# A mixture-of-experts tail in a language-model tower: coefficients applied in the expert blocks, block table computed one stage earlier

## The chip, the cores and the metric

The kernel runs on one core of a Trainium2 chip. The metric is the device time of one execution in microseconds (us). The engines are TensorE (PE in the profile, PEld its weight loads), VectorE (DVE), ScalarE (ACT), GpSimd (POOL) and SyncE (SP), which here only issues DMAs. On-chip memory is SBUF (128 partitions), matrix products land in the banks of PSUM, and everything that is passed between stages through memory outside the core goes through scratch tensors (`scratch_...`).

## The reference

Eight sequences of 512 tokens are embedded, run through a two-layer tower with banded attention, then through an induced-set attention block, and last through a two-level mixture of experts, which is the part that matters here:

```python
x = inp.reshape(-1, d)                     # 4096 tokens, d = 128
gw = _topk_gate(x @ wg_group, GK, G)       # 2 of 4 groups
z = _layernorm(x, ln_g, ln_b)
for g in range(G):
    iw = _topk_gate(z @ wg_inner[g], EK, E)    # 2 of 8 experts
    moe = jnp.zeros_like(z)
    for e in range(E):
        h = jax.nn.relu(z @ W1[g, e] + b1[g, e])
        moe = moe + iw[:, e:e + 1] * (h @ W2[g, e] + b2[g, e])
    y = _layernorm(z + moe, gln_g[g], gln_b[g])
    out = out + gw[:, g:g + 1] * y
return out + inp
```

Each token thus needs four expert rows, two for each of its two groups. The two of a group, weighted, and z are summed before a layernorm.

## The kernel before, in words

Four stages follow one another, each with its own program on every engine and a barrier between them: `embed`, `tower`, `induce`, `experts`. The change touches the last two.

**`induce`** works on eight items (sequences) in a software pipeline: a list of steps (`STEPS`), with 16 steps between items, and each engine runs for every step the pieces that are due in it. For an item m the gate is computed in the steps GATE to SLOT: VectorE's `coefficients` writes for each token its four expert coefficients and the 2 x 4 mixing weights of its groups into one tile `coef`, and `slots` the row of the scratch tensor `zs` for each of its four copies. GpSimd writes z and the token's number (column E) into the tile `z` with four copies of each token, and scatters them, 16 indirect DMAs for each item (L1440), so that the rows of one expert lie together in `zs`, in a region of its own. SyncE stores base, z and coef of each item to scratch tensors (L1375 to L1379). After the last item VectorE casts the counts of rows per expert (L1925), and SyncE and ScalarE write padding rows behind each region; GpSimd waits at the end for all scatters.

**`experts`** first loads constants (L1984), the coefficients (L1985), and on VectorE turns the counts into a table `tab` by a chain of 20 small operations (L2143 to L2164): for each of 95 blocks of 256 rows its expert and its first row in `zs`. Meanwhile TensorE transposes the mixing weights of all tokens (L2058), and ScalarE copies them to `mixed` (L2104). SyncE then goes through the blocks: two register loads from the table, a load of the expert's weights `w` (578 KB, six buffers) and one of the 256 rows (`rows`, 132 KB, six buffers, each reused when the scatter of six blocks before has landed). After block 4 (`if q == 4`) it also loads z and base of all tokens, 2 MB each.

For a block, TensorE transposes the rows (L2065), multiplies by W1 (L2077) and by W2 (L2089, one block behind). ScalarE copies the transposed rows (L2109) and applies bias and relu to one half of the hidden features (L2118), VectorE to the other (L2173). VectorE adds b2 (L2181) and GpSimd scatters the 256 results, two indirect DMAs (L2030), to `yt`, four rows for each token. The rows are not yet weighted.

When all scatters have landed, the **end** goes over the eight sequences, with two buffers `res` and two tiles `m`. SyncE loads the four result rows of each token (1 MB a sequence). VectorE multiplies rows 0 and 1 by their coefficients (L2190), GpSimd rows 2 and 3 (L2040). VectorE adds the two rows of each group (L2194) and z (L2195) and takes the statistics (L2201, L2204). GpSimd forms scale and shift in four small operations (L2043 to L2049), ScalarE normalises (L2129). TensorE multiplies the mixing weights with the group norms' gains and offsets (L2097); VectorE multiplies and adds (L2212, L2213, L2218, L2219), in the function `mixed_in`, which runs one sequence behind `gathered`.

Engines wait for each other by semaphores that count; `step` on VectorE waits for the operation just issued. PSUM banks go round in rings (`Tiles`) in an order that is a list of keys: in `up` the mixing keys stood first.

## Time and profile before

| | us |
|---|---|
| median of 3 runs | 2460.18 (2458.41 to 2463.89) |
| the profiled execution, its own time | 2446.1 |
| its span, first to last instruction | 2444.3 |
| TensorE busy in the span | 2019.2 (83%) |
| VectorE busy | 1323.6 (54%) |
| ScalarE busy | 1130.3 (46%) |
| GpSimd busy | 779.1 (32%) |

The profile is of one execution; its times are us from its first instruction. Busy time says how much an engine does, not whether anybody waits for it; that is read stage by stage, from windows of the span, and from a timeline: a list of instructions in order of time, merged where alike, with the idle time before each in brackets and what ended it. In a timeline `SPq` is the issue of a DMA by SyncE. The granted clock of TensorE is given as a share of 2.4 GHz: 0.50 is 1.2 GHz. The mean over the span is 0.88.

### The profile page before, as it was taken

The page shows a single profiled execution, that of the slowest core. Times are in us where ns is not written, and L with a number is a line of the kernel's source. Part 1 is how long each engine was busy: PE and PEld are TensorE (multiplying, and loading weights), DVE is VectorE, ACT ScalarE, POOL GpSimd, SP SyncE. Part 2 cuts the span into 40 slices and gives each one's busy share as a digit, 9 for nine tenths or more (in the row PEclk, how much of TensorE's full clock was granted, in tenths as well). Part 3 has the DMA queues.
Part 4 walks back from the last instruction along what each step waited for, and adds up shares of the span by engine and source line. Part 5 has one row for each costly group of instructions (what it writes and reads, how often), then busy time and mean ns, then how long its engine had stood idle before and what let it go on. Part 6 is the DMA issues. An engine that isn't in the chain of part 4 may idle for free. (4 is left out here: it accounts for less than half of the span.)

```text
span 2444.3 us, 43805 instructions
## 1 busy us (share of the span) xinstructions
PE 2019.2 (83%) x14601; PEld 1450.0 (59%) x14601; DVE 1323.6 (54%) x4329; ACT 1130.3 (46%) x2400; POOL 779.1 (32%) x975
## 2 busy tenths in 40 slices
PE   5799999999999999999995478867665179999944
PEld 4466666666666666666664356645443069999922
DVE  2365556656566555665562455776755223333358
ACT  2476656666666666665661134544432023333322
POOL 0012222222221222212222111235667625555543
PEclk7699999999999999999997566987776589999965
DMA  3641344213442144412400334522311477777622
GB/s 99 121 75 34 40 66 66 54 30 51 66 66 69 22 65 66 66 40 28 66 2 0 84 75 81 100 60 58 77 32 50 134 244 229 232 230 215 194 93 79
DMA packets 119393, 211.47 MB, mean 87 GB/s; under 512 B 23236, under 2 KB 52038, under 8 KB 118520
## 3 DMA queue, kind: packets, MB, share of 16 engines
q1 hardware_dynamic: 108024, 189.29, 34.9%
q0 software_dynamic: 10176, 17.09, 2.1%
q8 instruction: 124, 2.03, 0.4%
q10 hardware_dynamic: 976, 2.30, 0.3%
q14 instruction: 93, 0.76, 0.1%
HBM read 149.82 MB, written 66.82 MB: 89 GB/s over the span
## 5 line engine op out<-in xcount | busy, mean ns | idle before, releaser
L675 ACT ACTIVATE tower_prob<-tower_prob,tower_negmax 128x386 f32<-128x386 f32 (+1 forms) x768 | 390.5, 556 | 303.1 <-DVE tower_negmax L882 302.5
L882 DVE CUSTOM_DVE_ANT_0 tower_prob<-tower_sbank,tower_band 128x386 f32<-128x386 f32 (+1 forms) x768 | 346.4, 489 | 138.1 <-PE tower_sbank L449 132.9
L487 PEld LDWEIGHTS tower_tbank<-tower_ident,tower_prob 128*128 128x128 f32 x1920 | 227.6, 143 | 131.1 <-issue 81.0
L487 PE MATMUL tower_tbank<-tower_ident,tower_prob 128*128 128x128 f32 x1920 | 283.9, 278 | 23.2 <-DVE tower_probT L907 21.2
L731 ACT ACTIVATE tower_probT<-tower_tbank 128x384 f32<-128x384 f32 (+1 forms) x576 | 228.0, 431 | 126.3 <-PE tower_tbank L487 124.0
L2030 POOL DMA_INDIRECT scratch_yt<-experts_y,experts_rows x190 | 186.7, 983 | 202.4 <-DVE experts_y L2181 171.7
L426 PE MATMUL tower_dbank<-tower_oxT,tower_w 96*128 96x512 f32 x384 | 192.0, 625 | 12.1 <-ACT tower_oxT L720 12.0
L2089 PE MATMUL experts_ybank<-experts_w,experts_hid 128*128 128x128 f32 x1520 | 186.8, 277 | 0.0
L2118 ACT ACTIVATE experts_hid<-experts_hbank,experts_w 128x256 f32<-128x256 f32 x190 | 79.8, 471 | 224.4 <-PE experts_hbank L2077 224.4
L2077 PE MATMUL experts_hbank<-experts_zT,experts_w 128*128 128x256 f32 x760 | 182.1, 383 | 1.0 <-issue 1.0
L449 PE MATMUL tower_sbank<-tower_k_st,tower_q_st 49*128 49x386 f32 (+1 forms) x768 | 160.5, 412 | 26.3 <-POOL tower_k_st L631 13.6
L2089 PEld LDWEIGHTS experts_ybank<-experts_w,experts_hid 128*128 128x128 f32 x1520 | 178.9, 193 | 0.1
L2173 DVE TENSOR_SCALAR experts_hid<-experts_hbank,experts_w 128x256 f32<-128x256 f32 x190 | 83.2, 480 | 144.1 <-PE experts_hbank L2077 144.1
L647 POOL TENSOR_TENSOR tower_glob<-tower_vglob,tower_prob 128x102 f32<-128x102 f32 x128 | 46.5, 364 | 351.3 <-ACT tower_prob L675 227.5
L2077 PEld LDWEIGHTS experts_hbank<-experts_zT,experts_w 128*128 128x128 f32 x760 | 138.6, 193 | 16.9 <-issue 1.7
L346 PE MATMUL tower_dbank<-tower_w,tower_hid 128*128 128x192 f32 x768 | 140.7, 334 | 4.5 <-DVE tower_hid L857 4.5
L466 PE MATMUL tower_obank<-tower_probT,tower_v 128*17 128x128 f32 x3840 | 142.6, 275 | 0.7 <-ACT tower_probT L731 0.7
L1440 POOL DMA_INDIRECT scratch_zs<-induce_z,induce_slot x128 | 127.2, 994 | 38.4 <-issue 38.1
L365 PE MATMUL tower_dbank<-tower_xT,tower_wqk 96*96 96x512 f32 x256 | 131.9, 642 | 5.5 <-ACT tower_xT L690 5.5
L346 PEld LDWEIGHTS tower_dbank<-tower_w,tower_hid 128*128 128x128 f32 x768 | 123.1, 190 | 17.8 <-issue 10.9
L449 PEld LDWEIGHTS tower_sbank<-tower_k_st,tower_q_st 49*128 49x128 f32 x768 | 74.1, 185 | 94.4 <-issue 83.4
L1506 ACT ACTIVATE induce_probT<-induce_tbank 128x512 f32<-128x512 f32 x128 | 69.6, 597 | 96.8 <-PE induce_tbank L1145 56.3
(315 smaller groups left out, 3397.2 us busy)
## 6 DMA issues: line engine op xcount, KB each, us to landing
experts_w<-ew SPq DMA_DIRECT2D x95, 578.0 KB, 4.0
scratch_qk<-tower_qk SPq DMA_DIRECT2D x64, 384.0 KB, 4.7
tower_q_st<-scratch_qk SPq DMA_DIRECT2D x96, 192.0 KB, 8.2
tower_k_st<-scratch_qk SPq DMA_DIRECT2D x96, 192.0 KB, 11.2
experts_rows<-scratch_zs SPq DMA_DIRECT2D x95, 132.0 KB, 3.1
scratch_kq<-induce_kq SPq DMA_DIRECT2D x8, 1024.0 KB, 4.3
experts_res<-scratch_yt SPq DMA_DIRECT2D x8, 1024.0 KB, 5.6
induce_k_st<-scratch_kq SPq DMA_DIRECT2D x48, 128.0 KB, 4.3
```

The source lines that it names most:

```text
L346: mm = pe.matmul(bank[:, j * D:(j + 1) * D], lhs[:, k, t * P:t * P + P], rhs[:, k, :], start=(k == 0), stop=(k == kts - 1))
L365: mm = pe.matmul(bank[0:DP, :], wqk[layer][:, w, k, c * DP:c * DP + DP], xT[:, k, :], start=(k == 0), stop=(k == KT - 1))
L426: mm = pe.matmul(bank[:, :], w1[:, k, c * P:c * P + P], oxT[:, k, :], start=(k == 0), stop=(k == KT - 1))
L449: mm = pe.matmul(bank[:, 0:width(i)], stack(q_st[j], h0 + e)[:, i * P:i * P + P], stack(k_st[j], h0 + e)[:, first_key(i):first_key(i) + wi ...
L466: mm = pe.matmul(obank[32 * e:32 * e + W17, c:c + P], v[nq % 2][:, t, h0 + e, :], probT[(2 * gq + e) % PT][:, jb * P:jb * P + P], start=(j ...
L487: mm = pe.transpose(bank[:, jb * P:jb * P + P], prob[:, hg % PR, at + jb * P:at + jb * P + P], ident[:, :])
L675: act.activation(prob[:, hg % PR, 0:width(i)], prob[:, hg % PR, 0:width(i)], ACT.Exp, bias=negmax[:, hg % PR:hg % PR + 1], scale=-1.0).the ...
L731: turned.copied(act.activation(probT[(2 * (g - 1) + e) % PT][:, 0:at], bank[:, 0:at], ACT.Copy), ("t", g - 1, e))
L882: scores.copied(dve.tensor_tensor_reduce(prob[:, hg % PR, 0:width(i)], bank[:, 0:width(i)], band[:, BAND_AT[i]:BAND_AT[i] + width(i)], sca ...
L2030: pool.indirect_dma_start(out=a["yt"], out_offset=bass.IndirectOffsetOnAxis(ap=rows[q % ZB][:, h, E:E + 1].bitcast(U32), axis=0), in_=y[q ...
L2077: mm = pe.matmul(bank[:, j * TB:j * TB + TB], w[q % WW][:, W1 + c * P:W1 + c * P + P], zT[q % 2][:, :], start=True, stop=True)
L2089: mm = pe.matmul(bank[:, h * E:h * E + E], hid[q1 % 2][:, c, h * P:h * P + P], w[q1 % WW][:, W2 + c * E:W2 + c * E + E], start=(c == 0), s ...
```

## The change

Three things are done.

1. The four coefficients of a token travel with its rows: `coefficients` writes them to column E + 1 of the tile `z`, before the scatter. In a block, ScalarE forms half of the row's z (`zhalf`), and VectorE, after adding b2, forms y * coefficient + zhalf with two scalar_tensor_tensor, one for each 128 rows. A new semaphore `y_set` says that this is done; the scatter waits for it. The sum of a group's two rows then contains weights and z. z is no longer stored and loaded.
2. The block table is computed at the end of `induce`, behind the cast of the counts (L1925), with its constants loaded among that stage's late loads; table, counts and identity lie in tiles that outlive the stages. The mixing weights are loaded after block 4 and transposed after the last block.
3. At the end GpSimd alone adds the two rows of each group (`pair_sums`), one sequence ahead; there are four `res` buffers and three `m` tiles. VectorE keeps the statistics and the mixing.

The core of the diff (the 20 operations of the table are moved as they are):

```diff
@@ induce: coefficients on VectorE @@
-                    ins = dve.tensor_tensor(coef[:, :, SLOTS + j * G:SLOTS + j * G + G], outer_(hot),
+                    ins = dve.tensor_tensor(coef[:, :, j * G:j * G + G], outer_(hot),
                                             weights(4 - j)[:, :, G:G + 1].broadcast_to([P, NT, G]), ALU.mult)
-                step(ins)
-                dve.tensor_reduce(coef[:, :, 0:SLOTS], parts[:, :, :, :], AX.X, ALU.add).then_inc(coef_set, 1)
+                ins.then_inc(gates_set, 1)
+                dve.wait_ge(gates_set, m + 1)
+                dve.wait_ge(z_named, m + 1)
+                dve.tensor_reduce(z[m % 2][:, :, :, E + 1], parts[:, :, :, :], AX.X, ALU.add).then_inc(coef_set, 1)
@@ induce: stores on SyncE @@
-                        sp.wait_ge(z_ready, m + 1)
-                        sp.dma_start(a["z"][m], z[j][:, :, 0, 0:E]).then_inc(z_out, 16)
-                        sp.wait_ge(coef_set, m + 1)
+                        sp.wait_ge(gates_set, m + 1)
                         sp.dma_start(a["coef"][m], coef[:, :, :]).then_inc(coef_out, 16)
@@ induce: scatter on GpSimd @@
                             pool.wait_ge(z_copied, m + 1)
+                            pool.wait_ge(coef_set, m + 1)
...
-                            pool.wait_ge(z_out, 16 * (m - 1))
@@ induce: late loads @@
-                (grows, "grows"), (wgate, "wgate"), (rank, "rank"), (upper, "upper"), (ids, "ids0"))
+                (grows, "grows"), (wgate, "wgate"), (rank, "rank"), (upper, "upper"), (ids, "ids0"),
+                (steps, "steps"), (tri, "tri"), (origin, "count0"), (bidx, "iota"))
@@ induce: end of VectorE @@
             dve.tensor_copy(tail[:, :], count[0:1, :]).then_inc(tail_set, 1)
+            step(dve.tensor_tensor(blocks[:, :], count[:, :], origin[:, :], ALU.subtract))
...
+            dve.tensor_copy(tab[:, :], tabf[:, :]).then_inc(tab_set, 1)
+            dve.wait_ge(tab_set, 1)
@@ experts @@
-        WW, ZB, YB = 6, 6, 4
+        WW, ZB, YB, RB, MB = 6, 6, 4, 4, 3
...
-        res = [ph.sb(f"res{j}", [P, TC, SLOTS, E]) for j in range(2)]
-        m = [ph.sb(f"m{j}", [P, TC, 2, E]) for j in range(2)]
+        res = [ph.sb(f"res{j}", [P, TC, SLOTS, E]) for j in range(RB)]
+        m = [ph.sb(f"m{j}", [P, TC, 2, E]) for j in range(MB)]
...
-            for dst, src in consts:
-                sp.dma_start(dst[:], a[src]).then_inc(consts_in, 16)
-            sp.dma_start(coef[:, :, :].rearrange("p (r t) c -> p r (t c)", r=B),
-                         a["coef"].rearrange("r p t c -> p r (t c)")).then_inc(coef_in, 16)
-            sp.wait_ge(tab_set, 1)
             for q in range(NBLK):
...
                 if q == 4:
-                    sp.dma_start(z[:, :, :].rearrange("p (b t) d -> p b (t d)", b=B),
-                                 a["z"].rearrange("b p t d -> p b (t d)")).then_inc(base_in, 16)
+                    sp.dma_start(glmix[:, :], a["glmix"]).then_inc(consts_in, 16)
+                    sp.dma_start(coef[:, :, :].rearrange("p (r t) c -> p r (t c)", r=B),
+                                 a["coef"].rearrange("r p t c -> p r (t c)")).then_inc(coef_in, 16)
@@ experts: ScalarE, in each block @@
+                act.wait_ge(rows_in[q % ZB], 16 * (q // ZB + 1))
+                if q >= 2:
+                    act.wait_ge(y_set, q - 1)
+                act.activation(zhalf[q % 2][:, :, :], rows[q % ZB][:, :, 0:E], ACT.Copy, scale=0.5)\
+                    .then_inc(zhalf_set, 1)
@@ experts: VectorE, in each block @@
+                    down.wait_copied(dve, ("y", q1))
+                    dve.wait_ge(zhalf_set, q1 + 1)
+                    for h in range(HB):
+                        yh = y[q1 % YB][:, h, :]
+                        ins = dve.scalar_tensor_tensor(yh, yh, rows[q1 % ZB][:, h, E + 1:E + 2],
+                                                       zhalf[q1 % 2][:, h, :], ALU.mult, ALU.add)
+                    ins.then_inc(y_set, 1)
@@ experts: GpSimd, in each block @@
-                down.wait_copied(pool, ("y", q))
+                pool.wait_ge(y_set, q + 1)
@@ experts: GpSimd, the end @@
-            pool.wait_ge(coef_in, 16)
+            def pair_sums(b):
+                pool.wait_ge(res_in[b % RB], 16 * (b // RB + 1))
+                if b >= MB:
+                    pool.wait_ge(added, b - MB + 1)
+                pairs = res[b % RB][:, :, :, :].rearrange("p t (j k) d -> p t j k d", k=2)
+                pool.tensor_tensor(m[b % MB][:, :, :, :], pairs[:, :, :, 0, :], pairs[:, :, :, 1, :], ALU.add)\
+                    .then_inc(summed, 1)
+            pair_sums(0)
             for b in range(B):
-                pool.wait_ge(res_in[b % 2], 16 * (b // 2 + 1))
-                part = res[b % 2][:, :, 2:SLOTS, :]
-                pool.tensor_tensor(part, part, coef[:, TC * b:TC * b + TC, 2:SLOTS, None]
-                                   .broadcast_to([P, TC, 2, E]), ALU.mult).then_inc(scaled, 1)
+                if b + 1 < B:
+                    pair_sums(b + 1)
                 pool.wait_ge(moments, b + 1)
@@ experts: VectorE, the end (gathered) @@
-                dve.wait_ge(res_in[b % 2], 16 * (b // 2 + 1))
-                part = rb[:, :, 0:2, :]
-                step(dve.tensor_tensor(part, part, coef[:, TC * b:TC * b + TC, 0:2, None].broadcast_to([P, TC, 2, E]),
-                                       ALU.mult))
-                dve.wait_ge(scaled, b + 1)
-                pairs = rb[:, :, :, :].rearrange("p t (j k) d -> p t j k d", k=2)
-                step(dve.tensor_tensor(mb[:, :, :, :], pairs[:, :, :, 0, :], pairs[:, :, :, 1, :], ALU.add))
-                dve.tensor_tensor(mb[:, :, :, :], mb[:, :, :, :],
-                                  z[:, TC * b:TC * b + TC, None, :].broadcast_to([P, TC, 2, E]), ALU.add)\
-                    .then_inc(summed, 1)
                 dve.wait_ge(summed, b + 1)
```

Two places show how instructions move. The first is SyncE's program at the start of `experts`, before (constants, then `experts_tab` is read into registers):

```order
L1984 DMA experts_ident<-ident 128x128
L1984 DMA experts_glmix<-glmix 8x384
L1984 DMA experts_steps<-steps 128x16
L1984 DMA experts_tri<-tri 128x1024
L1984 DMA experts_origin<-count 128x32
L1984 DMA experts_bidx<-iota 128x1
L1985 DMA experts_coef<-scratch_coef 128x8x48
L1989 TENSOR_LOAD experts_tab
...
L1990 TENSOR_LOAD experts_tab
...
L1993 DMA experts_w<-ew 128x1156
```

and the same place with the change, where the table is called `sh_tab` (the last row of `induce` stands first):

```order
L1058 DMA scratch_zs<-padrows 16x2112
L924 UNCONDITIONAL_BRANCH
L2007 UNCONDITIONAL_BRANCH
L2010 TENSOR_LOAD sh_tab
...
L2011 TENSOR_LOAD sh_tab
...
L2014 DMA experts_w<-ew 128x1156
...
L2018 DMA experts_rows<-scratch_zs 128x264
```

Seven loads have gone from in front of the first weights. The second place is VectorE's program for one round of the end, before:

```order
L2190 TENSOR_TENSOR experts_res<-experts_res,experts_coef 128x4x256
L2194 TENSOR_TENSOR experts_m<-experts_res 128x1024
L2195 TENSOR_TENSOR experts_m<-experts_m,experts_z 128x1024
L2201 BN_STATS experts_st<-experts_m 128x6 x8
L2204 BN_AGGR experts_mv<-experts_st 128x2 x8
L2212 TENSOR_TENSOR experts_out<-experts_out,experts_hbank 128x128
```

and with the change, on VectorE and then, for one round, on GpSimd:

```order
L2222 TENSOR_TENSOR experts_out<-experts_out,experts_m 128x512
L2204 BN_STATS experts_st<-experts_m 128x6 x8
L2207 BN_AGGR experts_mv<-experts_st 128x2 x8
L2215 TENSOR_TENSOR experts_out<-experts_out,experts_hbank 128x128
L2216 TENSOR_TENSOR experts_m<-experts_m,experts_hbank 128x256
```

```order
L2064 TENSOR_TENSOR experts_m<-experts_res 128x1024
L2072 TENSOR_SCALAR experts_rstd<-experts_mv 128x8
L2074 TENSOR_TENSOR experts_rstd<-experts_rstd,experts_half 128x8
L2076 TENSOR_TENSOR experts_shift<-experts_rstd,experts_mv 128x8
L2078 TENSOR_SCALAR experts_shift<-experts_shift 128x8
```

Three operations of 1024 elements have left VectorE's round, and GpSimd's multiplication of that size has become the pair sum, which stands before the four small operations of the sequence one back.

## Rows read from the trace of the kernel before

**Rows 1.** Windows of blocks and of the end; first line names the columns
```profile
core 0: us, PE busy (x) PEld busy (x) DVE busy (x) ACT busy (x) POOL busy (x), PEclk, DMA share, GB/s
...
2000.00:2100.00 100.00, 100.00 (x699) 93.17 (x698) 34.70 (x80) 33.07 (x81) 52.90 (x54) 1.00 0.70 220
...
2345.00:2445.00 100.00, 38.38 (x56) 17.41 (x56) 84.61 (x232) 25.48 (x64) 40.38 (x40) 0.50 0.29 90
```
**Rows 2.** Timeline at the boundary: start us, duration us, engine, line, [idle before]
```profile
1913.45 0.16 DVE L1925 CAST induce_tail<-count 1x32 int32<-1x32 f32 x1
...
1944.39 0.96 POOL L1440 DMA_INDIRECT scratch_zs<-induce_z,induce_slot  x1 [0.30 <-issue]
...
1948.54 0.35 SPq L1984 DMA_DIRECT2D experts_ident<-ident  x1
...
1961.10 0.17 DVE L2164 CAST experts_tab<-experts_tabf 128x2 int32<-128x2 f32 x1
...
1962.77 0.38 SPq L1993 DMA_DIRECT2D experts_w<-ew  x1
...
1966.91 0.69 PE L2065 MATMUL experts_zbank<-experts_ident,experts_rows 128*128 128x128 f32 x2 [6.85 <-DMA experts_rows<-scratch_zs]
```
**Rows 3.** Timeline around the two large loads issued after block 4
```profile
1972.84 0.43 SPq L2000 DMA_DIRECT2D experts_z<-scratch_z  x1
...
1991.34 0.69 PE L2065 MATMUL experts_zbank<-experts_ident,experts_rows 128*128 128x128 f32 x2 [5.41 <-DMA experts_rows<-scratch_zs]
...
1997.32 0.38 PE L2065 MATMUL experts_zbank<-experts_ident,experts_rows 128*128 128x128 f32 x2
```
**Rows 4.** Windows of two stretches, columns as in rows 1
```profile
1952.00:1954.00 2.00, 0.00 (x0) 0.00 (x0) 0.20 (x2) 0.00 (x0) 0.00 (x0) 0.50 0.87 219
...
1986.00:1988.00 2.00, 0.00 (x0) 0.00 (x0) 0.88 (x2) 0.03 (x1) 1.46 (x2) 1.00 1.05 412
```
**Rows 5.** DMA issues in 1970 to 1995: count, KB each, us to landing
```profile
experts_z<-scratch_z SPq DMA_DIRECT2D x1, 2048.0 KB, 10.8
```
**Rows 6.** Timeline of one steady expert block
```profile
2326.23 0.88 DVE L2173 TENSOR_SCALAR experts_hid<-experts_hbank,experts_w 128x256 f32<-128x256 f32 x2 [1.41 <-PE experts_hbank L2077]
...
2326.35 0.38 ACT L2109 ACTIVATE experts_zT<-experts_zbank 128x256 f32<-128x256 f32 x1 [0.16 <-PE experts_zbank L2065]
...
2328.13 0.43 DVE L2181 TENSOR_TENSOR experts_y<-experts_ybank,experts_w 128x256 f32<-128x256 f32 x1 [1.03 <-PE experts_ybank L2089]
```
**Rows 7.** Timeline: VectorE's L1892 beside GpSimd, twice
```profile
1755.66 2.05 DVE L1892 SCALAR_TENSOR_TENSOR induce_gc<-induce_ga,induce_gates 128x160 f32<-128x160 f32 x1
...
1756.25 1.27 POOL L1483 TENSOR_TENSOR induce_base<-induce_h,induce_x 128x512 f32<-128x512 f32 x1
...
1903.47 1.03 POOL L1440 DMA_INDIRECT scratch_zs<-induce_z,induce_slot  x1 [0.30 <-issue]
...
1903.70 0.33 DVE L1892 SCALAR_TENSOR_TENSOR induce_gc<-induce_ga,induce_gates 128x160 f32<-128x160 f32 x1
```
**Rows 8.** Timeline of the end: first item, one round, last item
```profile
2344.57 1.23 DVE L2190 TENSOR_TENSOR experts_res<-experts_res,experts_coef 128x1024 f32<-128x1024 f32 x1 [10.71 <-DMA experts_res<-scratch_yt]
...
2377.59 2.41 POOL L2040 TENSOR_TENSOR experts_res<-experts_res,experts_coef 128x1024 f32<-128x1024 f32 x1
...
2378.17 2.92 DVE L2190 TENSOR_TENSOR experts_res<-experts_res,experts_coef 128x1024 f32<-128x1024 f32 x1
...
2383.64 1.64 DVE L2201 BATCH_NORM_STATS2 experts_st<-experts_m 128x6 f32<-128x128 f32 x8
...
2385.88 0.25 DVE L2212 TENSOR_TENSOR experts_out<-experts_out,experts_hbank 128x128 f32<-128x128 f32 x1
...
2389.01 3.18 ACT L2129 ACTIVATE experts_m<-experts_m,experts_shift,experts_rstd 128x128 f32<-128x128 f32 x8 [8.17 <-POOL experts_shift L2049]
...
2389.52 2.92 DVE L2190 TENSOR_TENSOR experts_res<-experts_res,experts_coef 128x1024 f32<-128x1024 f32 x1
...
2437.89 0.29 DVE L2212 TENSOR_TENSOR experts_out<-experts_out,experts_hbank 128x128 f32<-128x128 f32 x1 [2.63 <-ACT experts_m L2129]
```

More of the change, by code:

```diff
@@ L1 @@
+from collections import namedtuple
 from contextlib import ExitStack
@@ L74, in clear @@
         pool.drain().then_inc(self.go, 1)
+Shared = namedtuple("Shared", "count tab ident")
 class Chain:
@@ L912, in _, with induce @@
             ph.leave(dve)
-def induce(nc, a, outer, count, xs):
+def induce(nc, a, outer, shared, xs):
     with ExitStack() as ctx:
@@ L1382, in _ @@
             pad_regions(sp, 0)
-            for sem in (base_out, z_out, coef_out):
+            for sem in (base_out, coef_out):
                 sp.wait_ge(sem, 16 * B)
@@ L2092, in _ @@
                     down.filled(mm, ("y", q1))
+            pe.wait_ge(consts_in, 16)
+            pe.wait_ge(coef_in, 16)
+            for b in range(B):
+                bank = up.claim(pe, ("mix", b))
+                for t in range(TC):
+                    mm = pe.transpose(bank[0:2 * G, t * P:t * P + P], coef[:, TC * b + t, :], ident[:, :])
+                up.filled(mm, ("mix", b))
             for b in range(B):
@@ L2101, in _ @@
         def _(act):
-            for b in range(B):
-                bank = up.take(act, ("mix", b))
-                up.copied(act.activation(mixed[:, b * S:b * S + S], bank[0:2 * G, :], ACT.Copy), ("mix", b))
             def turned(q):
```

135 lines of the change are left out of this document (62 added, 73 removed).

## The prediction

> **What bounds the kernel now.** I read the windows by stage first, to see which engine fills each stage that the change touches; then the timelines at the stage boundaries, to see what is waited for there.
>
> The 95 expert blocks are TensorE's alone: in the window of 2000 to 2100 it is busy 100 of 100 us at a granted clock of 1.00 (2.4 GHz), while VectorE has 34.70 and ScalarE 33.07 us of work [rows 1]. The end is not TensorE's: from 2345 to 2445 VectorE is busy 84.61 of 100 us and TensorE's clock is at 0.50 (1.2 GHz), of no weight there [rows 1]. So work that leaves VectorE's end shortens the span, and work that is put under the blocks is free as long as it fits beside TensorE.
>
> Between the stages nobody computes. The last scatter of rows is issued at 1944.39, the expert stage begins at 1948.54 with a load of constants, the block table is written at 1961.10, the first expert's weights are asked for at 1962.77 and TensorE starts at 1966.91 [rows 2]. A second hole is inside the blocks: at 1991.34 TensorE had idled 5.41 us for the rows of block 5 [rows 3], which stand in the queue behind two loads of 2 MB (z and base) that were issued after block 4's.
>
> **The change, part by part.**
>
> *Start of the expert stage.* Constants, table and the ScalarE and TensorE work on the mixing weights leave the front. Six loads, the coefficient load and the chain of 20 VectorE operations go from between 1948.54 and 1961.27. In their place SyncE does what it does today between the written table and the first load, two register loads: 1962.77 - 1961.27 = 1.50 us at most, with the wait in it [rows 2]. The first weights are then asked for at 1948.54 + 1.50 = 1950.04, **12.7 us earlier**; the rest of the start (4.1 us to the first transpose) is as now. The 20 operations now stand behind the cast at 1913.45 and take, at today's pace, the 7.5 us from 1953.76 to 1961.27, so they end near 1921; the last scatter is issued at 1944.39 and the stage cannot end before it [rows 2]. That cover of 23 us would have to go wholly before the table costs anything. The four constant loads (0.5 MB, the triangle) that are added at the front of the stage before stand behind everything that stage needs early; I count them at nothing, and between -3 and +3 us for that whole stage, where also eight stores of z fall away.
>
> *The hole at block 5.* Issued after block 4 are now the mixing coefficients and base, no longer z. z's 2,048 KB [rows 5] at the 412 GB/s that flowed while TensorE waited [rows 4] are 5.1 us. Against that stand the coefficients, many small packets, today at the front: at most the 0.87 x 2 = 1.7 us that the queues were busy in 1952 to 1954 [rows 4]. The rows of block 5 thus land 5.1 - 1.7 = 3.4 us earlier and 5.41 - 3.4 = 2.0 us of waiting stay. The wait also cost the clock: the block after it takes 1997.32 - 1991.34 = 5.98 us [rows 3] where a steady one takes 0.88 + 1.03 + 0.43 + 1.41 = 3.75 by VectorE's own work and idle time [rows 6], so 2.2 us were lost at 1.2 GHz: the same pair of transposes takes 0.69 us there and 0.38 later [rows 3]. A wait of 2.0 us should not lose the clock, as it was still 1.00 in 1986 to 1988, after TensorE had stopped [rows 4]. Gain **5.6 us**, between 3.4 (clock lost all the same) and 7.6 (no wait left).
>
> *The blocks.* Per block VectorE gets two scalar_tensor_tensor of 128x128 from SBUF and two waits. The nearest row is the same operation on 128x160, 0.33 us [rows 7]; two are 0.66, with handoffs 0.75. They go into the gap behind the bias addition, which is 1.41 us long until the next hidden half arrives [rows 6], so 0.66 us of slack remain and TensorE is never kept waiting. ScalarE gets one 128x256 operation, like its 0.38 us copy [rows 6]: some 27 blocks per 100 us make 10 us on top of 33.07 [rows 1]. I take **0** for 95 blocks. Behind the new wait stand the scatters on GpSimd, 0.75 us later each, and behind them the reuse of the row buffers, six blocks deep; only the last scatter counts: **+0.7 us** before the results are read back.
>
> What the two sums share with GpSimd: beside the issue of a scatter VectorE's operation kept its 0.33 us, beside a GpSimd tensor_tensor of 1.27 us it took 2.05 [rows 7]. The scatters are all that GpSimd does in the blocks. The Trainium skill (SBUF — State Buffer, "Who interferes with whom") says that a VectorE instruction with two SBUF inputs contends with any GpSimd instruction that reads SBUF, and one of them blocks fully. By the 0.33 us the issue of a scatter is not such an instruction; by the rule alone it might be, and that case is the third rival below.
>
> *The end.* Now a round of one item takes 2389.52 - 2378.17 = 11.35 us, all VectorE's: scaling 2.92 (1.23 alone; it waits for GpSimd's 2.41 beside it), then pair sum and z, then statistics from 2383.64 to 2385.88 (G = 2.24) and mixing and adding to 2389.52 (M = 3.64) [rows 8]. Scaling, pair sum and z go: 11.35 - 2.24 - 3.64 = 5.5 us an item. VectorE's round becomes G + M + two handoffs = 6.0. But there is a second loop. The pair sum now is GpSimd's (2.41 as its multiplication of the same size), writes one of three tiles, and so waits until the item three back is added. For item b: pair sum of b+1 with handoff 2.5, the four small root operations from the end of statistics to ScalarE's start, 2389.01 - 2385.88 = 3.13, ScalarE's eight normalisations 3.18 (3.25 with handoff), M 3.64 [rows 8]: 12.5 us for two items, 6.26 each. The longer of the two is taken: 6.2 us. The first item is added after 2.5 + 2.24, then up to 5.0 for GpSimd's second pair sum, + 3.13 + 3.25 + 3.64 = 15.0; seven more rounds make 15.0 + 7 x 6.2 = 58.4. Today it is from 2344.57 to 2437.89 + 3.64 = 2441.53, 97.0 us [rows 8]. Gain **38.6 us**. All four result loads may be asked for at once, but the first is still first in the queue, so I leave its landing. The transposes of mixing weights that came from the front now stand between the last block and the mixing; VectorE idles 10.71 us there for the first results [rows 8], and the first mixing comes 11 us after that, so they are covered.
>
> *Sum.* -12.7 - 5.6 + 0.7 - 38.6 = **-56 us**. The profiled execution took 2446.1 us (span 2444.3), which would become 2390; the median of the runs shown is 14 us above it, 2460.2, and becomes 2404.
>
> **The rivals.**
>
> *Statistics wait for GpSimd.* The pair sum of b+1 runs exactly beside the statistics of b. If these wait for the whole 2.41, as VectorE's scaling does today (2.92 against 1.23 [rows 8]), G becomes 4.65, VectorE's round 8.4, and the end 17.3 + 7 x 8.3 = 75: 17 us are given back, 2421. For it: the scaling row. Against: scaling reads two SBUF tensors, statistics one; nowhere before do the two meet, so no row tells. The Trainium skill (same page and section) says that one SBUF input outside the two-port modes does not contend. Chance 0.08.
>
> *The start is not freed.* If the stage cannot begin its loads without something else that today hides under the constants (fetching its code, the first wait), up to 12.7 us stay: 2417. Nothing in the rows shows such a thing: the first instruction at 1948.54 comes at once. Chance 0.05.
>
> *Slower: the scaling stalls the blocks.* If each scalar_tensor_tensor waits for the issue of a scatter (1.03 us [rows 7]), VectorE's addition is 2 x (0.33 + 1.03) = 2.7 us in a gap of 1.41, the next hidden half is 1.3 us late, and TensorE waits for it in each of 95 blocks: +124 us, in all 2404 + 124 = 2528. It decides from 56 / 95 = 0.6 us of lateness a block, an addition of 2.0 us. For it: GpSimd issues two scatters in every block, and a tensor_tensor there did stretch the same operation to 2.05. Against: the 0.33 beside a scatter [rows 7]. Chance 0.05.
>
> *The change does little.* If the end were bound by the reading back of results and not by VectorE, its 38.6 would shrink. 8 MB at 412 GB/s are 20 us of 58; against it. With other mishaps that leave the time within 0.2%: 0.02.
>
> **How the numbers follow.** Forecast as worked out: 0.80. Its own range is 2404 with -2 and +2 for block 5, -3 and +3 for the stage before, some -4 to +4 in the handoffs of the end, and the 3 us by which the runs shown differ: 2393 to 2415. To hold 8 in 10 with the first two rivals in part, the range is 2392 to 2420. A measurement of this kernel can tell about 0.2%, 5 us. Faster: 0.80 + 0.08 + 0.05 = 0.93; within 0.2%: 0.02; slower: 0.05.
>
> **What would show it.** Right: the first weight load some 1.5 us after the stage's first instruction; a wait before block 5 of 2 us with the clock kept; TensorE 100 of 100 us busy in the blocks and VectorE near 34.7 + 27 x 0.66 = 52; rounds of 6.2 us in the end, with GpSimd's pair sum released by the adding of the item three back. Wrong: statistics longer than 2.3 us beside the pair sum; hidden halves that VectorE hands over late; TensorE's idle time between blocks. A time above 2420 would say that one of these happened, one below 2392 that the stage before, which I hold at nothing, gained from the stores that left.

## The result and the profile after

The changed kernel took 2405.3 us in the median of 4 runs (2399.7 to 2409.8), the kernel before beside it 2460.8 us (4 runs, 2458.4 to 2463.9): a ratio of 0.9773, 95% interval 0.9749 to 0.9796. Forecast were 2404 us and a range of 2392 to 2420.

The profiled execution took 2404.6 us, near its own median, while that of before took 2446.1, 14 us under its median. So the two profiles differ by 41.5 us and the medians by 55.5. The 14 us between them are no gain or loss of the change; where they lie is the first thing to find.

The windows of the changed kernel, the blocks and the end from the first sum of result rows to the last add; then the end of before, cut in the same way:

```profile
core 0: us, PE busy (x) PEld busy (x) DVE busy (x) ACT busy (x) POOL busy (x), PEclk, DMA share, GB/s
2000.00:2100.00 100.00, 100.00 (x700) 93.18 (x699) 51.19 (x135) 41.01 (x108) 52.45 (x54) 1.00 0.76 236
...
2341.66:2400.03 58.37, 38.37 (x56) 17.39 (x56) 46.09 (x208) 25.48 (x64) 39.94 (x40) 0.50 0.46 152
```

```profile
2344.57:2441.53 96.96, 38.38 (x56) 17.41 (x56) 84.92 (x232) 25.48 (x64) 40.79 (x40) 0.50 0.30 92
```

In the blocks VectorE went from 34.70 us [rows 1] to 51.19 and ScalarE from 33.07 to 41.01, and TensorE is still busy in all 100 us at 2.4 GHz: the added work is free there. The end went from 97.08 us (its last add ends at 2440.96 + 0.69 = 2441.65, 0.12 us behind the window above, which is cut at the end that the prediction had worked out) to 58.37. VectorE's work in the two windows went from 84.92 to 46.09. That the smaller work alone does not bring the shorter end is shown below by the run with two tiles.

The boundary of the stages in the changed kernel (start us, duration us, engine, line). It answers to [rows 2]:

```profile
1916.64 0.16 DVE L1937 CAST induce_tail<-sh_count 1x32 int32<-1x32 f32 x1
...
1917.84 40.88 ACTq L1058 DMA_DIRECT2D scratch_zs<-padrows  x16
...
1918.85 41.44 SPq L1058 DMA_DIRECT2D scratch_zs<-padrows  x16
...
1924.04 0.17 DVE L1959 CAST sh_tab<-induce_tabf 128x2 int32<-128x2 f32 x1
...
1945.29 0.96 POOL L1451 DMA_INDIRECT scratch_zs<-induce_z,induce_slot  x1 [0.30 <-issue]
...
1962.97 0.10 POOL L2046 MEMSET experts_half<- 128x8 f32 x1 [16.73 <-POOLq L924]
...
1964.27 0.38 SPq L2014 DMA_DIRECT2D experts_w<-ew  x1
...
1968.58 0.69 PE L2086 MATMUL experts_zbank<-sh_ident,experts_rows 128*128 128x128 f32 x2 [58.12 <-DMA experts_rows<-scratch_zs]
```

The table is done at 1924.2, long before it is needed, and the first weights are asked for 1.30 us after the stage's first instruction (the memset), where before it was 14.23 (1948.54 to 1962.77 [rows 2]). But the stage itself begins 17.7 us behind the last scatter, not 4.15. What ends late are the padding writes behind each region of `zs`: 16 on each of two queues, in 41 us. In the profile of before they took half of that, here on SyncE's queue:

```profile
1914.76 20.44 SPq L1046 DMA_DIRECT2D scratch_zs<-padrows  x16
```

### The profile page after: what moved, and what is told of

Its sections match the earlier page's. It is cut to its first block and busy times, and to the rows that moved or that the text cites. A ratio compares the mean times of both kernels' runs of the same rounds, so it can differ in the third digit from the quotient of the medians.

```text
span 2402.7 us, 44240 instructions
## 1 busy us (share of the span) xinstructions
PE 2019.5 (84%) x14601; PEld 1445.8 (60%) x14601; DVE 1340.1 (56%) x4495; ACT 1156.6 (48%) x2495; POOL 778.4 (32%) x975
```

## The experiments

Each run below has the kernel before beside it, on the same chip. Eight runs (the kernel before, the first repeat of the changed kernel, the table, four tiles, the extra load, the two with more operations and the six padding writes) were on one chip, the other four on another, which matters, as will be seen. On which chips the executions of the section above ran is not on record. Several experiments differ from the changed kernel by less than their 95% intervals; what they show is then read from the stage in the trace, and the text says so. Theory 1: the start, the hole and the end gained what was forecast, and the long padding writes have nothing to do with the change. Theory 2: the table, moved beside the scatters, makes the padding writes long, and most of the start's 12.7 us is given back.

**The kernel before, once more.** No edit.

> The kernel before, looked at again. Theory 1: the 32 padding writes at the end of the induce stage (L1046, issued from two queues beside GpSimd's scatters) take 20 us in some executions and 40 in others, whatever the kernel, and the first profiled execution of before (20 us, 2446.1 us in all, 14 under its median) was a short one; this look then often shows some 34 to 41 us for them, the expert stage 10 us or more behind the last scatter, and about 2460 us in all. Theory 2: the moved block table makes them slow; then they take 20 us here again and the expert stage begins 3 to 5 us after the last scatter.

Measured: 2462.7 us. The padding writes took 38.5 and 39.3 us, and the stage began 14.9 us behind the last scatter, all without the change:

```profile
1920.67 0.16 DVE L1925 CAST induce_tail<-count 1x32 int32<-1x32 f32 x1
...
1921.88 38.48 ACTq L1046 DMA_DIRECT2D scratch_zs<-padrows  x16
...
1922.86 39.33 SPq L1046 DMA_DIRECT2D scratch_zs<-padrows  x16
...
1949.64 0.96 POOL L1440 DMA_INDIRECT scratch_zs<-induce_z,induce_slot  x1 [0.30 <-issue]
...
1964.53 0.34 SPq L1984 DMA_DIRECT2D experts_ident<-ident  x1
...
1978.97 0.38 SPq L1993 DMA_DIRECT2D experts_w<-ew  x1
...
1983.25 0.69 PE L2065 MATMUL experts_zbank<-experts_ident,experts_rows 128*128 128x128 f32 x2 [6.41 <-DMA experts_rows<-scratch_zs]
```

One execution with the long writes and without the change is enough: theory 2 falls as the main cause. The part that the change touches reads as in [rows 2]: 18.7 us from the stage's first instruction to the first transpose.

**The changed kernel, twice more.** No edit; once on each chip.

> The changed kernel again, as the measure for the others on the same chip: about 2405 us, 0.977 of before. Theory 1: the padding writes take anything from 20 to 41 us, and the stage's start behind the last scatter follows them. Theory 2: they take about 40 us again.

> The changed kernel once more, as the measure for the three others on the same chip: 0.977 to 0.978 of before, about 2404 us; first sum of result rows to the last add 58.4 us.

Measured: 2403.8 us on the first chip (before 2457.6; ratio 0.9777, 0.9764 to 0.9791) and 2386.4 on the second (before 2446.0; 0.9756, 0.9739 to 0.9773). The boundary on the second chip:

```profile
1913.17 0.16 DVE L1937 CAST induce_tail<-sh_count 1x32 int32<-1x32 f32 x1
...
1914.36 19.74 ACTq L1058 DMA_DIRECT2D scratch_zs<-padrows  x16
1914.46 20.27 SPq L1058 DMA_DIRECT2D scratch_zs<-padrows  x16
...
1943.95 0.96 POOL L1451 DMA_INDIRECT scratch_zs<-induce_z,induce_slot  x1 [0.31 <-issue]
1948.09 0.10 POOL L2046 MEMSET experts_half<- 128x8 f32 x1 [3.18 <-POOLq L924]
1949.39 0.37 SPq L2014 DMA_DIRECT2D experts_w<-ew  x1
...
1953.61 0.69 PE L2086 MATMUL experts_zbank<-sh_ident,experts_rows 128*128 128x128 f32 x2 [46.63 <-DMA experts_rows<-scratch_zs]
```

The padding writes are quick here, with the change in. In the seven profiles from the first chip in which two queues issue all 32, the padding took 37 to 43 us; in the three from the second it took 20 to 21. I call these long and short padding. The executions can now be cut at the same five points and compared like with like (us, from starts in the timelines; the last add's end is its start + 0.69):

| from, to | before, short padding | after, short padding | before, long padding | after, long padding |
|---|---|---|---|---|
| start, cast of the counts | 1913.45 | 1913.17 | 1920.67 | 1914.86 |
| cast, stage's first instruction | 35.09 | 34.92 | 43.86 | 46.15 |
| that, first transpose | 18.37 | 5.52 | 18.72 | 5.53 |
| first transpose, first result sum or scaling | 377.66 | 371.96 | 377.99 | 373.58 |
| that, end of last add | 97.08 | 58.44 | 97.06 | 58.55 |
| the profiled execution | 2446.1 | 2388.5 | 2462.7 | 2403.2 |

With short padding the sum is -57.6 us: start -12.9, blocks -5.7, end -38.6, the rest -0.4. The first row is not the change's: with the table moved or not, the cast came anywhere from 1909.9 to 1920.7 in these runs.

**The table back at the start.** The table's four constants and its 20 operations go back; ident, coefficients and mixing stay where the change put them.

```diff
 # induce, VectorE
-            step(dve.tensor_tensor(blocks[:, :], count[:, :], origin[:, :], ALU.subtract))
...
-            dve.tensor_copy(tab[:, :], tabf[:, :]).then_inc(tab_set, 1)
 # experts, SyncE
+            for dst, src in ((steps, "steps"), (tri, "tri"), (origin, "count0"), (bidx, "iota")):
+                sp.dma_start(dst[:], a[src]).then_inc(tabc_in, 16)
+            sp.wait_ge(tab_set, 1)
 # experts, VectorE
+            dve.wait_ge(tabc_in, 64)
+            step(dve.tensor_tensor(blocks[:, :], count[:, :], origin[:, :], ALU.subtract))
...
+            dve.tensor_copy(tab[:, :], tabf[:, :]).then_inc(tab_set, 1)
```

> The changed kernel with the table's four small constants and its 20 VectorE operations put back at the start of the expert stage; the rest of the change stays. Theory 1 (the start gave the 12.7 us that were forecast, or somewhat less since ident and the coefficients stay out of the front): first weights asked for some 11 to 14 us behind the stage's first instruction instead of 1.4, time 2405 + 9 to 13 = 2414 to 2418. Theory 2 (the table beside the scatters makes the padding writes slow): these take 20 us again and give back 14 to 20 us, so the time is 2405 - 7 to 2405 + 0.

Measured: 2413.4 us, 0.9816 (0.9803 to 0.983), 9.6 us above the changed kernel on the same chip, as theory 1 had it (9 to 13). The padding writes still took 37.3 and 39.3 us. In the trace the first weights are asked for 13.25 us behind the memset instead of 1.30, a difference of 11.95:

```profile
1962.86 0.10 POOL L2025 MEMSET experts_half<- 128x8 f32 x1 [13.03 <-POOLq L924]
...
1976.11 0.36 SPq L1993 DMA_DIRECT2D experts_w<-ew  x1
```

Of the 2.3 us between that and 9.6, 1.1 lie in the blocks (first transpose to first result sum 372.45 against 373.58 us). The rest may be a small grain of theory 2: from the cast to the stage took 43.9 and 43.0 us in the two profiles on this chip with the table in the old place, and 43.9 to 46.8 in the five with only it moved and all writes on two queues. One execution of each kernel does not settle it. With short padding there is nothing of the kind (35.09 in the first profile of before, 34.4 to 34.9 in three with the table moved).

**A second large load after block 4.**

```diff
+                    sp.dma_start(extra[:, :, :].rearrange("p (b t) d -> p b (t d)", b=B),
+                                 a["base"].rearrange("b p t d -> p b (t d)")).then_inc(base_in, 16)
                     sp.dma_start(out[:, :, :].rearrange("p (b t) d -> p b (t d)", b=B),
...
-            dve.wait_ge(base_in, 16)
+            dve.wait_ge(base_in, 32)
```

> The changed kernel with one more load of 2 MB (base a second time, into a tile that nobody reads) put behind block 4's, where the load of z stood before. Theory 1 (the second 2 MB was the hole at block 5: 5.1 us at 412 GB/s): TensorE waits 3 to 6 us for block 5's rows again and the block after it may run at half the clock, time +3.4 to +7.6 us, 2407 to 2412. Rival (the hole came from the order of things at the old start, where TensorE had its first weights earlier than the rest): no wait or one under 1 us, time unchanged.

Measured: 2408.3 us (0.9796, 0.9778 to 0.9815), 4.5 above the changed kernel's run on that chip, whose interval overlaps this one (0.9764 to 0.9791), so the trace has to decide. TensorE idles before block 5 as in [rows 3]:

```profile
1989.42 0.69 PE L2088 MATMUL experts_zbank<-sh_ident,experts_rows 128*128 128x128 f32 x2 [7.06 <-DMA experts_rows<-scratch_zs]
```

From first transpose to first result sum it is 379.4 us (1963.20 to 2342.63) against 373.6 without the load: 5.9 us. From block 4's transposes to block 6's alone it is 16.3 us instead of 7.5. Theory 1 holds: the hole is what stands in the queue ahead of block 5's rows.

**Four, and eight, more operations on VectorE in every block.**

```diff
+                    for n in range(4):                       # 8 in the second
+                        dve.scalar_tensor_tensor(spare[:, n, :], zhalf[q1 % 2][:, n % HB, :],
+                                                 rows[q1 % ZB][:, n % HB, E + 1:E + 2],
+                                                 zhalf[q1 % 2][:, n % HB, :], ALU.mult, ALU.add)
                     for h in range(HB):
                         yh = y[q1 % YB][:, h, :]
```

> The changed kernel with four more scalar_tensor_tensor of the same form in every block on VectorE, written to a tile that nobody reads, ahead of the two real ones: 4 x 0.305 = +1.22 us of VectorE a block, where its next hidden half comes 0.76 us later. Theory A (as the rival of the prediction priced it: every us by which the hidden half is late is a us of TensorE): lateness 0.46 us x 95 = +44 us, 2448. Theory B (the hidden half of a block is needed only after the next block's first layer, some 2.8 us after VectorE hands it over, so VectorE counts only once its work fills the whole 3.74 us of a block; it now does 1.90, with these 3.12): no change but up to 1.2 us for the last scatter, 2404 to 2406, TensorE still 100 of 100 us busy.

> The same with eight more: 8 x 0.305 = +2.44 us a block, VectorE's work 1.90 + 2.44 = 4.34 us in a block of 3.74. Theory A (lateness of the hidden half counts in full): (2.44 - 0.76) x 95 = +160 us, 2564. Theory B (only VectorE's throughput counts): a block takes 4.34 us and up to 0.3 for handoffs, so +57 to +86 us, 2461 to 2490, VectorE busy over 90 of 100 us in the blocks and TensorE some 80 to 86. If these operations waited for the issues of GpSimd's scatters their mean would rise above 0.305.

Measured: 2400.3 us with four (0.9761, 0.9738 to 0.9784), 2417.0 with eight (0.9822, 0.98 to 0.9844). Windows of the first and of the second (same columns as above):

```profile
2000.00:2100.00 100.00, 100.00 (x700) 93.21 (x699) 77.60 (x243) 42.02 (x108) 53.49 (x54) 1.00 0.73 231
```

```profile
2000.00:2100.00 100.00, 97.13 (x671) 88.69 (x670) 98.88 (x336) 42.05 (x104) 51.80 (x52) 1.00 0.69 223
```

With four more a block still takes 3.74 us, and TensorE is not kept waiting in this window. First transpose to first sum is 373.5 us (1961.83 to 2335.37), the 373.6 of the changed kernel, but that they are so equal is chance: the second block is 1.8 us shorter, as the clock rises earlier, while TensorE waits 1.05 us before block 5 and the first result sum comes 20.3 us behind the last block's transposes instead of 19.3, the late last scatter that theory B allows. The 3.5 us by which the median is lower are not of the blocks and lie within the intervals. With eight VectorE is full; one block, from start to start of its work:

```profile
2252.21 0.87 DVE L2181 TENSOR_SCALAR experts_hid<-experts_hbank,experts_w 128x256 f32<-128x256 f32 x2
2252.99 0.41 DVE L2189 TENSOR_TENSOR experts_y<-experts_ybank,experts_w 128x256 f32<-128x256 f32 x1
2253.44 2.19 DVE L2195 SCALAR_TENSOR_TENSOR experts_spare<-experts_zhalf,experts_rows 128x128 f32<-128x128 f32 x8
2255.55 0.61 DVE L2200 SCALAR_TENSOR_TENSOR experts_y<-experts_y,experts_rows,experts_zhalf 128x128 f32<-128x128 f32 x2
2256.07 0.87 DVE L2181 TENSOR_SCALAR experts_hid<-experts_hbank,experts_w 128x256 f32<-128x256 f32 x2
```

Theory A falls (it had +44 and +160). Theory B has the mechanism but was too high for eight (+57 to +86 against +13 between the medians, and +16.5 from first transpose to first sum, 1964.14 to 2354.19): eight in a row take 2.19 us, not 2.44, and an operation starts before the one ahead has ended, so that the four groups of durations 0.87, 0.41, 2.19 and 0.61, 4.08 together, fill only 3.86 us from start to start. Neither is stretched by GpSimd's scatters, which are issued during half of each block (51.8 of 100 us).

**Four tiles m in the end, and two, instead of three.**

```diff
-        WW, ZB, YB, RB, MB = 6, 6, 4, 4, 3
+        WW, ZB, YB, RB, MB = 6, 6, 4, 4, 4     # 2 in the other
```

> The changed kernel with four tiles m in the end instead of three. My theory (the two-item loop over GpSimd, ScalarE and VectorE that waits for the item three back holds every second round at 7.1 us): the pair sum no longer waits for the adding of the item three back, rounds fall from 6.48 to about VectorE's own 6.0, time 3 us lower, 2402. Rival (GpSimd's chain of pair sum 2.34 and four small operations with their waits, and ScalarE's 3.2 us behind it, holds the round whatever the tiles): rounds stay 6.4 to 6.5, time unchanged within 1 us.

> The changed kernel with two tiles m in the end instead of three. Theory 1 (GpSimd's pair sum of item b+1 then waits until item b-1 is added, and the four small operations of item b stand behind it on GpSimd): a round is pair sum 2.4 + small operations 2.5 + ScalarE 3.3 + mixing and adding 3.6 = 11.8 us, so 15 + 7 x 11.8 = 98 us for the end instead of 58, time 2404 + 37 to 40 = 2441 to 2444, which gives back the whole 38.6 us that the end was forecast to gain. Rival (VectorE's own work sets the round, the tiles only smooth it): rounds 6.5 to 7.3, time +0 to +6, 2404 to 2410.

Four tiles measured 2407.3 us (0.9794, 0.9775 to 0.9814), 3.5 above the changed kernel on that chip. The intervals overlap, so the medians say only that no 3 us were won; in the trace the end took 62.8 us (2339.97 to 2402.79) instead of 58.55. Both expectations missed it. The pair sum does start earlier, and here is what it meets; first with four tiles, then with three:

```profile
2352.62 2.35 POOL L2064 TENSOR_TENSOR experts_m<-experts_res 128x1024 f32<-128x1024 f32 x1
...
2353.24 2.29 DVE L2221 TENSOR_TENSOR experts_out<-experts_out,experts_m 128x512 f32<-128x512 f32 x1
...
2355.56 0.69 DVE L2222 TENSOR_TENSOR experts_out<-experts_out,experts_m 128x512 f32<-128x512 f32 x1
```

```profile
2353.51 0.69 DVE L2221 TENSOR_TENSOR experts_out<-experts_out,experts_m 128x512 f32<-128x512 f32 x1
...
2354.84 1.64 DVE L2204 BATCH_NORM_STATS2 experts_st<-experts_m 128x6 f32<-128x128 f32 x8
...
2355.07 2.35 POOL L2064 TENSOR_TENSOR experts_m<-experts_res 128x1024 f32<-128x1024 f32 x1 [2.14 <-DVE experts_out L2222]
```

VectorE's add takes 2.29 us instead of 0.69 beside GpSimd's pair sum, and ends 0.6 us after it does; in two later rounds the add takes 2.82 us, and in two others it is GpSimd's pair sum that is stretched, to 2.87. Two rounds take 14.4 us instead of 13.0. With three tiles the pair sum waits for the last of these adds and then runs beside the statistics, which keep their 1.64. The Trainium skill (SBUF — State Buffer, "Who interferes with whom") says that a VectorE instruction with two inputs from SBUF contends with a GpSimd instruction that reads SBUF, and that one with at most one such input, outside the two-port modes, does not. These rows agree with that rule: the adds have two, the statistics one. The wait for the third tile looked like a cost, and in these two executions it is what keeps the two apart.

Two tiles measured 2421.9 us (0.9897, 0.988 to 0.9915), 35.4 above the changed kernel on the second chip (2386.4). A round takes 12.2 us, nearly as theory 1 had it with 11.8, and the end 92.4 us instead of 58.4:

```profile
2378.29 0.69 DVE L2222 TENSOR_TENSOR experts_out<-experts_out,experts_m 128x512 f32<-128x512 f32 x1
...
2379.13 2.34 POOL L2064 TENSOR_TENSOR experts_m<-experts_res 128x1024 f32<-128x1024 f32 x1 [7.16 <-DVE experts_out L2222]
...
2381.55 0.24 POOL L2072 TENSOR_SCALAR experts_rstd<-experts_mv 128x8 f32<-128x8 f32 x1
...
2384.19 1.26 ACT L2161 ACTIVATE experts_m<-experts_m,experts_shift,experts_rstd 128x128 f32<-128x128 f32 x3 [9.00 <-POOL experts_shift L2078]
```

The small operations of the sequence one back start only when the pair sum behind the wait is done, and ScalarE idles 9 us for them. Without the third tile nearly all that the end gained would be lost, although VectorE would have just as little to do.

**The pair sum on VectorE.**

```diff
 # GpSimd: pair_sums and its calls go; VectorE, gathered:
-                dve.wait_ge(summed, b + 1)
+                dve.wait_ge(res_in[b % RB], 16 * (b // RB + 1))
+                if b >= MB:
+                    dve.wait_ge(added, b - MB + 1)
+                pairs = res[b % RB][:, :, :, :].rearrange("p t (j k) d -> p t j k d", k=2)
+                dve.tensor_tensor(mb[:, :, :, :], pairs[:, :, :, 0, :], pairs[:, :, :, 1, :], ALU.add)\
+                    .then_inc(summed, 1)
+                dve.wait_ge(summed, b + 1)
```

> The changed kernel with the pair sum moved from GpSimd to VectorE (three tiles stay). Theory 1 (alone it is 1.23 us, as the scaling of the same size was in before when GpSimd did not work beside it): VectorE's round goes from 5.87 without waits (6.48 as it is) to 7.2, first item 1.1 us earlier, +4 us in all, 2408. Rival (it takes the 2.9 us that VectorE's scaling took in before): rounds 8.9, +16 us, 2420.

Measured: 2389.7 us (0.9771, 0.9755 to 0.9787), 3.3 above the changed kernel beside it, with overlapping intervals; in the trace the end took 63.4 us instead of 58.4. Rounds are 7.13 us:

```profile
2363.81 0.69 DVE L2217 TENSOR_TENSOR experts_out<-experts_out,experts_m 128x512 f32<-128x512 f32 x1
...
2364.42 1.22 DVE L2194 TENSOR_TENSOR experts_m<-experts_res 128x1024 f32<-128x1024 f32 x1
...
2370.94 0.69 DVE L2217 TENSOR_TENSOR experts_out<-experts_out,experts_m 128x512 f32<-128x512 f32 x1
```

So of the end's 38.6 us, handing the pair sum to GpSimd is worth some 5; the rest goes with the scaling and the adding of z, which went altogether, and with the added buffers. No run puts the scaling back alone, so these two are not told apart here. On VectorE alone the operation takes 1.22 us, half of GpSimd's 2.34.

**Padding writes on GpSimd**, the last 6, then the last 10, behind its scatters.

```diff
+            pool.wait_ge(tail_set, 1)
+            pad_regions(pool, range(XE - LAST, XE), padded_pool)     # LAST = 6, or 10
             for j in range(2):
                 pool.wait_ge(scattered[j], 16 * NT * SLOTS * B // 2)
```

> The changed kernel with the last 6 of the 32 padding writes taken from SyncE and ScalarE (16 each, now 13) and issued by GpSimd behind its last scatter. Theory 1 (the stage boundary is set by the two queues, which issue 6 to 8 padding writes each at 1.28 us after the scatters): the expert stage begins 3 x 1.28 = 3.8 us earlier, 2400. Rival (what slows the padding writes is any issue by GpSimd, so GpSimd's own six now slow the rest for another 6 to 8 us): no gain or a loss of up to 5 us, 2404 to 2409.

> As the variant in which GpSimd issues the last 6 padding writes behind its scatters, but with 10, SyncE and ScalarE having 11 each. Theory 1 (the two queues' writes behind the last scatter, 1.28 us each, set the stage's start): SyncE and ScalarE have 2 to 3 fewer to issue than with 6 and the stage begins 12 to 14 us after the last scatter instead of 16.6 to 17.7, time 2404 - 4 to 2404 - 6. Rival (GpSimd's ten writes become the last, at the 2 us that its queue took for some of the six): begins no earlier than with 6, 2400 to 2404.

Measured: with 6, on the chip with long padding, 2397.1 us (0.9748, 0.973 to 0.9766) against 2403.8 (0.9764 to 0.9791). That is better than either theory had it (2400, or 2404 to 2409), but the gain is not shown: the intervals just touch, the two were not taken in one series, and in the series of the six padding writes the kernel with four more operations a block, which can hardly be faster than the changed kernel itself, stood at 2400.3, within the noise of it. Nor does the trace help: the profiled execution was the slowest of its five (2405.1 us), and its stage begins 15.2 us behind the last scatter, where it is 14.0 to 18.4 with all writes on two queues. With 10, on the other chip, 2394.2 (0.9787, 0.9773 to 0.9801) against 2386.4: 7.8 us slower. Here the two queues' 11 writes each are done after 14 us, and GpSimd's ten come after its last scatter and behind everything:

```profile
1947.69 4.93 POOL L1061 DMA_DIRECT2D scratch_zs<-padrows  x10
1957.96 0.10 POOL L2052 MEMSET experts_half<- 128x8 f32 x1 [5.34 <-POOLq L924]
```

From cast to stage it is 41.9 us there instead of 34.9. The expectation was written for long padding, which this chip does not have, so neither theory was tested by it. No version was shown to beat the changed kernel on either chip.

## Why the prediction was right

**The start: forecast -12.7.** Measured -12.9 and -13.2 from the stage's first instruction to the first transpose (table above). The 20 operations end at 1924.2 under the scatters, 3.2 us later than "near 1921", as the cast was in that execution; from 1916.73 they take the 7.5 us forecast. That the padding writes, and not the last scatter, may set the stage's beginning was overlooked: [rows 2] do not contain them, and the sentence that the stage "cannot end before" the last scatter named only one of two bounds. It cost the forecast little, as both kernels suffer (from cast to stage 43.9 us before and 46.2 after with long padding).

**The hole at block 5: forecast -5.6, and +0.7 for the last scatter, together -4.9.** Measured from first transpose to first sum: -5.7 with short padding and -4.4 with long. With short padding the steps hold in detail. From block 4's transposes to block 6's it is 9.5 us instead of 15.3, which is -5.8; the first result sum comes 19.2 us behind the last block's transposes instead of 18.6, which is +0.5; the other -0.4 are a clock that rose earlier in the first two blocks, which nobody had forecast. The wait is 1.8 us (forecast 2.0) and keeps the clock, the pair of transposes behind it taking 0.44 us instead of 0.69:

```profile
1974.00 0.44 PE L2086 MATMUL experts_zbank<-sh_ident,experts_rows 128*128 128x128 f32 x2 [1.83 <-DMA experts_rows<-scratch_zs]
```

With long padding the near agreement is partly luck. In both profiles of the changed kernel no wait is left at all, which gives 8.1 us at the hole and not 5.6; but the clock comes up one block later (the first layer of the second block takes 3.74 us at 1.2 GHz, and 1.97 to 2.04 in before and with short padding), so that the first four blocks take 2.0 us more than in before and TensorE comes to block 5 about as late as its rows. With 1.0 for single longer blocks (below) and 0.7 for the last scatter, -8.1 becomes the -4.4 measured. What makes the clock rise later was not tested. The length of the padding does not decide it, and neither does how long TensorE had idled ahead of the first transpose: the four tiles, with long padding and 58.35 us idle, have the early clock and a wait of 0.85 us; the ten padding writes, on the second chip and with 53.57 us idle, have the late clock and no wait.

**The blocks: forecast 0.** Held in the main: the four extra operations show that nearly three times the added work costs a steady block nothing. Not quite everything is free, though. In the two profiles of the changed kernel with long padding a few single blocks take longer (in the one at 2403.2 us six, up to 4.31 us, about 1.0 us together), and with short padding, and in both profiles of before, none does. Ahead of the longest VectorE had idled 3.12 us before adding b2; the profile names no engine that released it, and it was not followed up. What was wrong is the price of the third rival, which counted every us by which the hidden half is late. The run with four adds 0.61 + 1.17 = 1.8 us in the gap of 1.41, by that count 0.4 us late and 37 us in 95 blocks, and the steady blocks do not grow; the one with eight adds 2.8, by that count 132 us, and costs 0.12 to 0.13 us a block and 4.1 us behind the last one (first result sum 23.4 us behind the last block's transposes instead of 19.3). The hidden half of a block is multiplied only after the first layer of the next one, so VectorE's throughput counts and not its lateness.

**The end: forecast -38.6, 58.4 us.** Measured 58.4 to 58.6, against 97.1 before: -38.5 to -38.7. First item added 14.8 us after the start (forecast 15.0: 2340.12 to 2354.93 on the first chip), seven more rounds in 43.7 (7 x 6.2 = 43.4). Inside that the average hides two things: rounds alternate between 5.87 and 7.11, 12.98 us for two (forecast loop 12.5), and the last is only 4.8, as no statistics stand in it. The pair sum waits for the adding of the item three back in every second round only, the longer one. The forecast put each round at 6.2 where its own loop gave 6.26, which would have made 58.8 us; the longer loop and the short last round then cancel, which is luck to within 1 us. The loop is longer since two of GpSimd's small operations are stretched beside VectorE's adds, from 0.20 and 0.25 us to 0.56 and 0.68:

```profile
2373.89 0.56 POOL L2076 TENSOR_TENSOR experts_shift<-experts_rstd,experts_mv 128x8 f32<-128x8 f32 x1
...
2374.54 0.68 POOL L2078 TENSOR_SCALAR experts_shift<-experts_shift 128x8 f32<-128x8 f32 x1
```

The first rival, statistics that wait for GpSimd, did not come about (1.64 us beside the pair sum). Its mechanism is real, but between other operations, as the four tiles showed. The second and third rivals are refuted by the start's row and by the eight extra operations. The fourth, an end bound by reading back the results, is refuted by the trace with 2403.2 us: there the second pair sum waits 0.53 us for its result rows and no later one waits for any.

**The level.** The profile of before was an execution with short padding, and its 2446.1 us lie within the runs of before on the second chip (2442.5 to 2452.3) and outside those on the first (2450.2 to 2463.8); its median, 2460.2, lies within the latter. The forecast gain of 56 us was put on the median, and that was right, as the change moves both kinds nearly alike: -57.6 us between the profiles with short padding, -59.5 between those with long, of which 5.8 are the cast's earlier time. Between the medians it is -55.5 in the result, -53.8 on the first chip and -59.6 on the second.

## What to carry to other kernels

A buffer ring is not only there to smooth: with two tiles a wait in front of the pair sum held up the small operations queued behind it and cost 35 us, with four the wait vanished, the pair sum ran into VectorE's adds and the end grew by 4 us; so list for every wait you add what is queued behind it, and for every wait you remove what will then run side by side. In a pipelined block, ask when the result of an engine is really needed: VectorE had room until it was full, not until it was late. And when a profile's own time lies outside the span of its kernel's other runs, profile the kernel once more before comparing.

## What the hardware showed unexpectedly

- The same 32 padding writes took 37 to 43 us on the first chip, in both kernels, and 20 to 21 us on the second, in the changed kernel (and 20 us in the first profile of before). On the first chip each of the two queues issues a write every 1.2 to 1.5 us once GpSimd's scatters are done; beside the scatters single steps take up to 7.9 us in the changed kernel and 6.6 in before. On the second every step is 1.2 to 1.7 us, scatters or not. Why was not found, nor whether it is the chip or something else that differed between the series. The medians of before differ by 12 to 13 us between the two (2457.6 and 2459.3; 2446.0).
- GpSimd's indirect scatters do not slow VectorE's operations with two SBUF inputs: 0.61 us for two of them, 2.19 for eight, beside scatters in half of the time. A pair sum by GpSimd does: 0.69 becomes 2.29 (four tiles).
- scalar_tensor_tensor operations of 128x128 in a row overlap: 0.305 us each in twos (0.61 for both), 0.27 in eights (2.19 for all), while a single one shows 0.35.
